# Keys and values of the second layer's windowed attention, made turned in four column tiles

## The reference

```python
q = (x @ Wq + bq).reshape(b, s, 16, 16).transpose(0, 2, 1, 3)
k = (x @ Wk + bk).reshape(b, s, 2, 16).transpose(0, 2, 1, 3)
v = (x @ Wv + bv).reshape(b, s, 2, 16).transpose(0, 2, 1, 3)
# k and v padded by 32 tokens at each end; query s sees keys s .. s + 63 of the padded rows
scores = jnp.einsum('bgrsd,bgswd->bgrsw', qg, k_win)
out = jnp.einsum('bgrsw,bgswd->bgrsd', softmax(scores), v_win)
return out @ Wo + bo
```

## Time and profile before

| | |
|---|---|
| time, median of 3 runs | 4317.69 us (4316.76 to 4327.96) |
| time of the profiled execution | 4321.57 us |
| span of the profiled execution | 4319.8 us |
| mean granted clock of TensorE | 0.963 |
| busy: TensorE matmul | 3980.5 us (92%), 39417 instructions |
| busy: VectorE | 3322.9 us (77%) |
| busy: ScalarE | 2849.1 us (66%) |
| busy: GpSimd | 2003.2 us (46%) |
| the stage of the change, blocks 0 to 7 | about 930 to 1015 us of the span |

### The profile page before, as it was taken

How to read it: one execution, slowest core, us unless ns; L and a number is a source line. 1 busy time by engine, 2 the same in 40 slices (tenths; PEclk the granted TensorE clock), 3 DMA queues, 4 the chain that set the end, 5 groups by cost and what they waited for, 6 DMA issues and landing times. The chain is left out here.

```text
span 4319.8 us, 100821 instructions
## 1 busy us (share of the span) xinstructions
PE 3980.5 (92%) x39417; PEld 2123.1 (49%) x39417; DVE 3322.9 (77%) x5680; ACT 2849.1 (66%) x4554; POOL 2003.2 (46%) x1898
## 2 busy tenths in 40 slices
PE   8899999988959757899999999999999999999897
PEld 4344444564538423354544445455454555555555
DVE  7899999686665569888888888886137888888586
ACT  5577777664553155888888888875125777777664
POOL 5222222251235635888888888886001222222332
PEclk9899999998979979899999999999998999999999
DMA  4211111105335345455565655654223222222100
GB/s 146 66 39 39 39 39 39 27 28 124 73 114 160 98 113 125 125 156 160 148 169 146 149 146 156 170 151 134 87 90 106 65 65 61 61 70 61 31 13 27
DMA packets 263805, 412.40 MB, mean 95 GB/s; under 512 B 52731, under 2 KB 139802, under 8 KB 263170
## 3 DMA queue, kind: packets, MB, share of 16 engines
q1 hardware_dynamic: 228966, 375.81, 32.1%
q0 software_dynamic: 6912, 18.88, 1.8%
q10 hardware_dynamic: 27456, 11.28, 1.2%
HBM read 351.85 MB, written 53.24 MB: 94 GB/s over the span
## 5 line engine op out<-in xcount | busy, mean ns | idle before, releaser
L2968 POOL TENSOR_TENSOR l_dbx<-l_u,l_bc 128x1024 f32<-128x1024 f32 x256 | 603.4, 2357 | 247.3 <-DVE banks L3489 84.3
L1169 DVE CUSTOM_DVE_ANT_0 banks<-banks,l3s_table 128x1024 f32<-128x1024 f32 x512 | 619.4, 1241 | 89.5 <-PE banks L1089 84.7
L1252 ACT ACTIVATE l3s_probs<-banks 128x512 f32<-128x512 f32 x1024 | 540.3, 595 | 204.1 <-PE banks L1118 100.8
L1164 DVE TENSOR_REDUCE l0s_peak<-banks 128x1 f32<-128x1024 f32 x512 | 605.3, 1214 | 58.3 <-PE banks L1089 57.9
L1252 ACT ACTIVATE l0s_probs<-banks 128x512 f32<-128x512 f32 x1024 | 535.7, 600 | 164.8 <-PE banks L1089 163.1
L3276 ACT ACTIVATE banks<-l_dt,l_decay 128x512 f32<-128x512 f32 x512 | 346.7, 687 | 221.6 <-DVE banks L3489 219.1
L2978 POOL TENSOR_TENSOR l_ys<-l_ys,l_hc 128x1024 f32<-128x1024 f32 x203 | 479.6, 2362 | 21.5 <-DVE l_hc L3500 21.4
L3150 PE MATMUL banks<-l_ha,l_ring 128*128 128x512 f32 x1024 | 446.6, 593 | 3.9 <-issue 3.9
L3150 PE MATMUL banks<-l_hb,l_ring 128*128 128x512 f32 x1024 | 443.1, 593 | 1.6 <-ACT l_hb L3241 0.8
L3489 DVE TENSOR_TENSOR_SCAN banks<-banks,l_carry,l_dbx 128x512 f32<-128x512 f32 x256 | 319.3, 1279 | 68.7 <-ACT banks L3276 61.8
L1089 PE MATMUL banks<-l3s_q_st,l3s_k_st 122*32 122x512 bf16 x4096 | 346.9, 381 | 4.8 <-ACT l3s_probs L1252 1.0
(11 more groups left out here) (531 smaller groups left out, 7166.9 us busy)
## 6 DMA issues: line engine op xcount, KB each, us to landing
l_bc<-l_bc_rows SPq DMA_DIRECT2D x256, 512.0 KB, 5.4
l_ring<-in_l2f_stream SPq DMA_DIRECT2D x176, 512.0 KB, 6.4
l3s_table<-bias_table SPq DMA_DIRECT2D x16, 960.0 KB
qk_parts<-l0s_probs SPq DMA_DIRECT2D x96, 128.0 KB, 2.4
qk_parts<-l3s_probs SPq DMA_DIRECT2D x32, 384.0 KB, 3.5
y_rows<-l1f_out_b SPq DMA_DIRECT2D x80, 128.0 KB, 1.7
l0s_q_st<-qk_parts SPq DMA_DIRECT2D x64, 96.0 KB
l0s_k_st<-qk_parts SPq DMA_DIRECT2D x64, 96.0 KB
```

What stands on the lines that cost most here:

```text
L1164: nc.vector.tensor_reduce(out=peak[:, b % 2, t:t + 1], in_=s1[t % 2], axis=AX, op=ALU.max, negate=True).then_inc(s1_used, 1)
L1169: nc.vector.tensor_tensor_reduce(out=s1[t % 2], in0=s1[t % 2], in1=rows, scale=1.0, scalar=LOW, op0=ALU.add, op1=ALU.max, accum_out=peak[: ...
L1252: nc.scalar.activation(columns(probs[b % 2][:, t, :], half * 512, (half + 1) * 512), scores, ACT.Exp, scale=scale).then_inc(s2_used, 1)
L2968: nc.gpsimd.tensor_tensor(dbx[:, at:at + 2], u[:, 2 * mh:2 * mh + 2], bc[:, load % BR, 0].unsqueeze(1).to_broadcast([P, 2, TB]), ALU.mult)\
```

## The change

Keys and values are both made turned (channels on partitions), in four column tiles of the TensorE array: tile k takes the 32 channels as weights and streams the 128 tokens of tile k, so that the output is 128 partitions (4 tiles of tokens x 32 channels) by 128 tokens. Keys, their rest and their parts are held as 128 x 128 in place of 32 x 512. The values' bias is now added by ScalarE with its copy into `v_t`; the product of a row of ones and the bias is gone. `v_t` is turned back by one 128 x 128 transposition a block into bank 7, where it has the form that values had before. The transposition of block n-1's values comes on TensorE behind the queries of block n, and ScalarE's copy of them into `v_f` behind the second part of block n's queries; the last ones stand at the end. Keys are stored by four DMAs a block, one a column tile, each of 32 rows x 3 parts x 128 tokens.

```diff
-        self.k_parts = [spare[0:self.KV, cells:cells + 3 * TB].rearrange("p (a t) -> p a t", a=3),
-                        s.sb("k_parts", [self.KV, 3, TB], BF16)]
+        self.k_parts = [spare[:, cells:cells + 3 * P].rearrange("p (a t) -> p a t", a=3),
+                        s.sb("k_parts", [P, 3, P], BF16)]
...
-        for part in range(3):
-            sp.dma_start(self.k_scratch[part, :, b, at:at + TB], self.k_parts[n % 2][:, part, :])\
-                .then_inc(self.k_stored[n % 2], 16)
+        for k in range(BT):
+            sp.dma_start(self.k_scratch[:, :, b, at + k * P:at + (k + 1) * P].rearrange("a d t -> d a t"),
+                         self.k_parts[n % 2][k * self.KV:(k + 1) * self.KV]).then_inc(self.k_stored[n % 2], 16)
...
-        q_bank, k_bank = chip.psum[:, 4:6, :], chip.psum[0:KV, 6, :]
+        q_bank, k_bank, vt_bank = chip.psum[:, 4:6, :], chip.psum[:, 6, 0:P], chip.psum[:, 6, P:2 * P]
...
         def _(pe):
+            def turn_values(n):
+                pe.wait_ge(v_kept, n + 1)
+                wait(pe, v_ready, n)
+                nc.tensor.transpose(chip.psum[:, 7, 0:P], v_t[:], chip.ident[:]).then_inc(v_turned, 1)
...
                 last.then_inc(q_done, 1)
+                if n:
+                    turn_values(n - 1)
                 if n < NB - 1:
                     pre.tensor(pe, n + 1)
                 if n == 0:
                     pe.wait_ge(post_ready, before + NB - 1)
                 wait(pe, k_used, n)
-                wait(pe, v_ready, n)
-                for c in range(KC):
-                    nc.tensor.matmul(k_bank, w[:, c, D:D + KV], xt[:, c, :], start=(c == 0), stop=(c == KC - 1))
-                nc.tensor.matmul(v_bank, chip.ones[0:1, :], bv[:], start=True, stop=False)
-                for k in range(BT):
+                wait(pe, v_kept, n)
+                for bank, at in ((k_bank, D), (vt_bank, D + KV)):
                     for c in range(KC):
-                        last = nc.tensor.matmul(v_bank[:, k, :], xt[:, c, k * P:(k + 1) * P], w[:, c, D + KV:D + 2 * KV],
-                                                start=False, stop=(k == BT - 1 and c == KC - 1))
+                        for k in range(BT):
+                            last = nc.tensor.matmul(bank[k * KV:(k + 1) * KV, :], w[:, c, at:at + KV],
+                                                    xt[:, c, k * P:(k + 1) * P], start=(c == 0), stop=(c == KC - 1))
                 last.then_inc(kv_done, 1)
+            turn_values(NB - 1)
...
         def _(act):
+            def keep_values(n):
+                act.wait_ge(v_turned, n + 1)
+                wait(act, v_stored[n % 2], 16 * (n // 2))
+                nc.scalar.copy(v_f[:, n % 2], v_bank).then_inc(v_ready, 1)
...
                 nc.scalar.activation(k_f[:], k_bank, ACT.Identity, bias=bk[:]).then_inc(k_used, 1)
-                wait(act, v_stored[parity], 16 * (n // 2))
-                nc.scalar.copy(v_f[:, parity], v_bank).then_inc(v_ready, 1)
+                wait(act, v_turned, n)
+                nc.scalar.activation(v_t[:], vt_bank, ACT.Identity, bias=bv[:]).then_inc(v_kept, 1)
                 wait(act, q_rested, n + 1)
                 nc.scalar.copy(q_parts[:, 1], q_rest[:]).then_inc(q_middle, 1)
+                if n:
+                    keep_values(n - 1)
                 wait(act, k_used, n + 1)
-                wait(act, k_stored[parity], n // 2 * 48)
+                wait(act, k_stored[parity], n // 2 * 64)
                 nc.scalar.copy(k_parts[:, 0], k_f[:]).then_inc(k_high, 1)
                 wait(act, k_rested, n + 1)
                 nc.scalar.copy(k_parts[:, 1], k_rest[:]).then_inc(k_middle, 1)
+            keep_values(NB - 1)
```

More of the change, by code:

```diff
@@ L2178, in wait_stored @@
             sp.wait_ge(self.q_stored[parity], 96 * count)
-            sp.wait_ge(self.k_stored[parity], 48 * count)
+            sp.wait_ge(self.k_stored[parity], 64 * count)
             sp.wait_ge(self.v_stored[parity], 16 * count)
@@ L2221, in __init__ @@
         self.k_scratch, self.v_scratch, KV = k_scratch, v_scratch, k_scratch.shape[1]
-        self.sources = w_in, b_in, k_bias, repeated(v_bias, BT)
+        self.sources = w_in, b_in, k_bias, v_bias
         self.w = s.sb("w", [P, KC, D + 2 * KV])
-        self.bq, self.bk, self.bv = s.sb("bq", [P, KC]), s.sb("bk", [KV, 1]), s.sb("bv", [1, BT, KV])
+        self.bq, self.bk, self.bv = s.sb("bq", [P, KC]), s.sb("bk", [P, 1]), s.sb("bv", [P, 1])
         self.zeros = s.sb("zeros", [P, P])
         self.pre = PreNorm(chip, s, head=head)
-        self.q_rest, self.k_rest = s.sb("q_rest", [P, KC * TB]), s.sb("k_rest", [KV, TB])
-        self.q_f, self.k_f = s.sb("q_f", [P, KC, TB]), s.sb("k_f", [KV, TB])
+        self.q_rest, self.k_rest = s.sb("q_rest", [P, KC * TB]), s.sb("k_rest", [P, P])
+        self.q_f, self.k_f, self.v_t = s.sb("q_f", [P, KC, TB]), s.sb("k_f", [P, P]), s.sb("v_t", [P, P])
+        self.v_kept, self.v_turned = s.sem("v_kept"), s.sem("v_turned")
         self.loaded, self.zeroed, self.ends_stored = s.sem("loaded"), s.sem("zeroed"), s.sem("ends_stored")
@@ L2251, in run @@
         k_high, k_rested, k_middle = self.k_high, self.k_rested, self.k_middle
-        v_f = stacks.v_f
+        v_f, v_t, v_kept, v_turned = stacks.v_f, self.v_t, self.v_kept, self.v_turned
         q_flat = q_f[:].rearrange("p c t -> p (c t)")
@@ L2588, in normalise @@
                     g.wait_ge(stacks.q_stored[0], 96 * (NB // 2))
-                    g.wait_ge(stacks.k_stored[0], 48 * (NB // 2))
+                    g.wait_ge(stacks.k_stored[0], 64 * (NB // 2))
                 rows = y[:, t, group * PER * HD:(group + 1) * PER * HD].rearrange("p (h d) -> p h d", d=HD)
@@ L3710, in layout @@
     a["l1_w"] = np.concatenate([np.asarray(i[f"L1_attn_W{n}"]) for n in "qkv"], axis=1)
-    a.update(l1_bq=np.asarray(i["L1_attn_bq"]).reshape(-1, P).T, l1_bk=np.asarray(i["L1_attn_bk"]).reshape(-1, 1),
-             l1_bv=row(i["L1_attn_bv"]), l1_wo=np.asarray(i["L1_attn_Wo"]), l1_bo=row(i["L1_attn_bo"]))
+    a.update(l1_bq=np.asarray(i["L1_attn_bq"]).reshape(-1, P).T, l1_bk=np.tile(np.asarray(i["L1_attn_bk"]), BT).reshape(-1, 1),
+             l1_bv=np.tile(np.asarray(i["L1_attn_bv"]), BT).reshape(-1, 1), l1_wo=np.asarray(i["L1_attn_Wo"]), l1_bo=row(i["L1_attn_bo"]))
     c, p = np.arange(P + 64)[None, :], np.arange(P)[:, None]
```

## The result

The kernel after takes 4328.41 us (median of 13 runs, 4325.88 to 4335.46), the kernel before 4320.67 beside it (13 runs). The ratio is 1.0018 with a 95% interval of 1.0010 to 1.0025: some 8 us slower (4 to 11), where 4312.4 was forecast and the range ended at 4322. The profiled span is 4326.6 us.

The account below looks back on a forecast made before the run. The prediction took a VectorE, ScalarE and GpSimd loop to bound the stage's blocks, and the SP queue to decide its end after the change, 5.3 us earlier: 4317.7 - 5.3 = 4312.4 us, range 4305 to 4322.

Parts of the forecast that it names:

- The loop of 9.14 us a block: Second layer's input stage: the cycle through VectorE, ScalarE and GpSimd falls from 10.30 to 9.14 us a block.
- The terms 0.40, 0.40 and 0.35: Savings per block with narrower keys: VectorE's L2380 and L2382 lose 0.40 us each, ScalarE's L2362 0.35.
- 32 matmuls in 1.28 us: TensorE in the input stage: a block's new key and value matmuls take 1.28 us, costed at nothing in blocks 0 to 6.
- idle time of 3.2 us a block: TensorE in the input stage: it would idle about 3.2 us in each block after the change.
- The rival in which TensorE falls to half clock: Input stage: idling keeps TensorE at half clock, 11.1 us a block, 4322 us in all; chance 0.05.
- the rival of slow small pieces: Input stage: key stores with 256-byte runs land in over 6.4 us and stop the loop; 4318 us, chance 0.03.
- VectorE's end 1006.2: End of the input stage: VectorE would finish at 1006.2 us, 9.0 us earlier than before.
- SyncE's 1009.9: End of the input stage: the SP queue's stores and loads end at 1009.9 us and end the stage; chance 0.56.
- 1.5 more: Last block of the input stage: VectorE ends a further 1.5 us earlier if the last queries run at full clock.
- The term -5.3 us: End of the input stage: SP ends it at 1009.9 in place of 1015.2 us, 5.3 us earlier.
- Forecast: 4317.7 - 5.3: Whole kernel: the stage's 5.3 us is taken off the median 4317.7, giving 4312.4 us.
- the gain is eaten behind the barrier: Attention after the stage: its start waits or TensorE's clock falls shift; 4316 to 4319 us, chance 0.14.

Follow-up runs that it names:

- before + 72: The kernel before with 36 small matmuls that compute nothing (72 TensorE instructions) at the end of the input stage; ratio 1.0009 to before.
- after + 144: The kernel after with 72 small matmuls that compute nothing (144 TensorE instructions) ahead of the last block's transposition; ratio 1.0018 to before.

## Why the prediction was wrong, point by point

- **The loop of 9.14 us a block**: 9.20. The terms 0.40, 0.40 and 0.35, by which the three steps were to shrink, came out as 0.39, 0.39 and 0.32 (0.28 and 0.29 us are left of them, and 0.30 of ScalarE's copy, L2376).
- **32 matmuls in 1.28 us, idle time of 3.2 us a block**: 1.08 and 3.27. The rival in which TensorE falls to half clock didn't come: from 970 to 980 us the granted clock is 1.00 in after, with idle times of 1.89 and 1.38 us beside it. Nor did the rival of slow small pieces: the key stores in the stage landed after 2.4 to 2.5 us (medians) in both kernels, and the key part that was to wait for them (L2374) starts without idle time.
- **VectorE's end 1006.2, SyncE's 1009.9, SyncE decides**: 1006.6 and 1011.2, and SyncE decides. That VectorE's end agrees is luck: the last queries ran at full clock (3.70 us), for which the prediction took off 1.5 more, and a wait that it didn't have gave as much back.

```profile
1001.08 1.04 ACT L2362 CAST l1s_q_parts<-l1q_q_f 128x1024 bf16<-128x1024 f32 x1 [1.56 <-DMA q_parts<-l1s_q_parts]
```

  Of SyncE's 1.3 us, 1.0 is there by the end of block 4's keys (991.1 against 990.1), the most of it one load of queries.

```profile
983.08 2.34 SPq L2187 DMA_DIRECT2D l1s_q_st<-q_parts  x3
```

  It was taken as 1.6. The four key stores take 1.87 to 2.03 us against 1.88. The later store of the values, with a stage 1.3 and 1.6 us shorter in the two kernels that have it, fits that SyncE ends it.
- **The term -5.3 us** is mis-sized. Against the profiled execution it measured -4.0. But that execution's last block ran its queries at half clock; the prediction noted this for the kernel after ("1.5 more") and took the kernel before as it stood. Two profiles each give meetings of 1013.6 and 1011.2 on average: -2.4. Counted from the stage's own first matmul, which came 0.7 us later in after, they give 87.6 and 84.6: -3.0, and only -2.0 against the profile of before whose last block ran at full clock.
- **The step that failed** is "Forecast: 4317.7 - 5.3": the attention and all behind it taken as unchanged. The rival "the gain is eaten behind the barrier" names the place and was given 0.14 and 4316 to 4319, a price without a mechanism. By two profiles each, first exp to last went from 141.9 to 146.0: +0.2 in chunks 0 to 9, +4.6 in chunks 10 to 23, -0.7 in the last eight. From the last exp to the end before needs 3156.3 and 3156.2, after 3159.0 and 3160.7: +3.6. With -1.8 up to the first exp that is +5.9, within the 4 to 11 that the runs show.
- **What is shown**: the place of the fetch decides the +4.6. It goes with 72 instructions more, comes with 184 in before, stays with 256, and is gone at 71 and 72 in both kernels. What a fetch at the bad place delays, the issues or TensorE itself, is not shown.
- **What stays open**: the +3.6 behind the attention, which single profiles don't settle, since the rest lies between 3156.2 and 3169.1 us over the 16 profiles and is 3164.6 in before + 72, without the change; what makes chunks 0 to 9 take 48 to 56 us, in the same kernel too; and therefore why after + 144 is as slow as after. The whole times of the kernels that leave the loads where they were, sorted by "code", agree between before and after within their intervals: 1.0013 to 1.0020 at 183 and 184, 0.9999 at 219 and 255, 1.0018 and 1.0009 at 71 and 72. So the place of the code may decide the whole of the loss, but in chunks 10 to 23 alone it is shown where it is paid.
- No version beat before. After with 36 or 72 instructions of padding has 0.9999 (0.9989 to 1.0008), some 8 us less than after, so what the stage gained is not to be told from nothing in the whole time.

## What to carry to other kernels

A change of 0.1% in one stage can be outweighed by where it pushes the code behind it: if TensorE's loop has about as many instructions as a fetch holds (here 257 to 260 and 256), the fetch comes at the same place of every turn. Before such a change is judged, add a few matmuls that do nothing ahead of the loop and see whether its period moves. And a forecast that subtracts from one profiled execution should look at the clock in the block it subtracts from; a second profile of the kernel before is worth more than a finer walk. And a stage is to be compared from its own start: of 2.9 us at the meeting, 1.7 had come about before it.

## What the runs showed of the hardware

Over the 16 profiles, in chunks 10 to 23, ScalarE's query-load issues by their distance to the nearest start of a 16,384-byte fetch of TensorE's code: under 0.5 us, 53 of 114 took over 0.9 us (mean 0.97); 0.5 to 1 us, 9 of 156 (mean 0.48); beyond 1 us, none of 388 (mean 0.48). The longest in after took 2.06 us, where the median is 0.48. So code loading for one engine can hold up the DMA issues of another. SyncE's issues seem to be held up less: in the same stretch one of them was above 0.9 us in after, and none in the other 15 profiles. I had not expected that the same kernel's stage would end 3.6 us apart in two executions either, 2.1 us of it with the last block, whose eight matmuls took 6.43 us at a granted clock of 0.50 and 3.70 at 1.00.
